# Attention and a quantised feed-forward layer on one core: the feed-forward work dealt between the attention steps of the next two batches

## The reference

```python
Q, K, V = (proj(Wq), proj(Wk), proj(Wv))              # einsum('oc,bct->bto'), split into heads
att = jnp.einsum('bhqd,bhkd->bhqk', Q, K) * (1.0 / math.sqrt(Dh)) + b[0]
att = att * m + (1.0 - m) * NEG_INF
att = jax.nn.softmax(att, axis=-1)
y = jnp.einsum('bhqk,bhkd->bhqd', att, V)             # transposed back to (B, C, T)
...
vals = NVFP4_LUT[idx] * scales                        # gate, up: [4096, 512], down: [512, 4096]
gate = jnp.einsum('th,nh->tn', xt, Wg)
up = jnp.einsum('th,nh->tn', xt, Wu)
gelu = jnp.tanh(0.7978845608028654 * (gate + 0.044715 * gate ** 3)) * gate * 0.5 + gate * 0.5
out = jnp.einsum('tn,hn->th', gelu * up, Wd)
return x + out.reshape(B, S, H)
```

## Time and profile before

| | us |
|---|---|
| median of three runs | 1612.29 |
| profiled execution, its own time | 1610.11 |
| span of its trace | 1608.3 |
| TensorE busy / VectorE / ScalarE / GpSimd | 1510.4 / 695.6 / 534.6 / 270.4 |
| mean granted TensorE clock | 0.937 |
| ScalarE table loads | 2, of 1283 ns |

### The profile page before, as it was taken

The page is one execution under the profiler, slowest core; times in us unless marked ns, Lnnn a source line. Parts: engine busy times, 40 slices in busy tenths (PEclk is TensorE's granted clock), DMA queues, the critical chain, the costliest instruction groups (busy, mean ns, idle before and its releaser), DMA issues.

```text
span 1608.3 us, 19482 instructions
## 1 busy us (share of the span) xinstructions
PE 1510.4 (94%) x7376; PEld 597.7 (37%) x7376; DVE 695.6 (43%) x1113; ACT 534.6 (33%) x701; POOL 270.4 (17%) x146
## 2 busy tenths in 40 slices
PE   3989889898989889999999999999999999999999
PEld 1222222222322224444444444444444444444444
DVE  5858676776777562323323233323233232122122
ACT  1447464564656463222222222222222222111111
POOL 2012112121211212122112212211221221000000
PEclk7779896897898899999999999999999999999999
DMA  5112221212221103001001000100100010000000
GB/s 165 44 51 59 65 63 43 61 44 57 67 69 42 51 21 124 20 20 40 20 20 33 26 20 20 39 20 20 36 23 20 20 39 1 0 26 26 0 26 26
DMA packets 32662, 63.04 MB, mean 39 GB/s; under 512 B 5584, under 2 KB 14928, under 8 KB 32480
## 3 DMA queue, kind: packets, MB, share of 16 engines
q1 hardware_dynamic: 29760, 59.42, 12.5%
q10 hardware_dynamic: 2848, 2.90, 0.5%
HBM read 49.43 MB, written 12.61 MB: 39 GB/s over the span
## 4 chain that ended last, share of the span: by engine, by line
PE 82%; DMA 6%; DVE 5%; SPq 3%; ACT 2%; issue 1%; ACTq 1%; POOL 1%; POOLq 0%; DVEq 0%
PE psum L828 14%; PE psum L830 14%; PE psum L829 14%; PE psum L769 7%; PE psum L899 7%; PE psum L901 7%; PE psum L900 7%; PE psum L798 6%; DMA wide<-seed_rows 4%; DVE maxima L638 3%; PE psum L784 3%; PE psum L756 2%; PE psum L805 1%; PE psum L746 1%; DMA wide<-max_lo 1%
## 5 line engine op out<-in xcount | busy, mean ns | idle before, releaser
L638 DVE TENSOR_REDUCE maxima<-psum 128x1 f32<-128x512 f32 x512 | 332.3, 685 | 161.9 <-PE psum L769 158.3
L703 DVE SCALAR_TENSOR_TENSOR small<-psum,small 128x512 f32<-128x512 f32 x128 | 88.5, 691 | 592.6 <-issue 306.6
L544 ACT ACTIVATE big<-psum 128x1024 f32<-128x1024 f32 x256 | 253.4, 1024 | 214.8 <-PE psum L784 198.2
L769 PE MATMUL psum<-wide 51*128 51x512 f16 x512 | 211.3, 447 | 68.3 <-DMA wide<-seed_rows 51.1
L580 ACT ACTIVATE small<-psum 128x512 f32<-128x512 f32 x128 | 76.4, 597 | 421.1 <-PE psum L830 421.1
L334 POOL TENSOR_TENSOR dq_w<-dq_code,dq_scales 128x1536 f32<-128x1536 f16 x32 | 109.8, 3433 | 541.8 <-DVE dq_code L371 541.8
L590 ACT CAST in_hi<-small 128x512 f16<-128x512 f32 x128 | 79.1, 618 | 361.8 <-DVE small L703 361.8
L828 PE MATMUL psum<-y_hi,wide 128*128 x512 | 194.1, 379 | 2.6 <-POOL wide L346 2.6
L828 PE MATMUL psum<-y_hi,w_even_hi 128*128 (+1 forms) x512 | 194.2, 379 | 1.2 <-POOL w_even_lo L346 1.2
L829 PE MATMUL psum<-y_lo,w_even_hi 128*128 (+1 forms) x512 | 194.0, 379 | 0.0
L830 PE MATMUL psum<-y_hi,w_even_lo 128*128 (+1 forms) x512 | 194.0, 379 | 0.0
(11 more groups left out here) (83 smaller groups left out, 1366.2 us busy)
## 6 DMA issues: line engine op xcount, KB each, us to landing
dq_packed<-packed SPq DMA_DIRECT2D x32, 384.0 KB
dq_scales<-scales SPq DMA_DIRECT2D x32, 384.0 KB
wide<-qk_parts SPq DMA_DIRECT2D x64, 128.0 KB
qk_parts<-wide SPq DMA_DIRECT2D x60, 128.0 KB
small<-x SPq DMA_DIRECT2D x8, 512.0 KB, 4.1
wide<-qk_parts SPq DMA_DIRECT2D x64, 64.0 KB
big<-x SPq DMA_DIRECT2D x4, 1024.0 KB, 9.5
out<-big SPq DMA_DIRECT2D x16, 256.0 KB, 2.1
```

The source lines that it names most:

```text
L544: nc.scalar.activation(p_exp[:, k, :, i], p_score[:, 2 * i:2 * i + 2, :], ACT.Exp, scale=SCORE_SCALE).then_inc(exp_done, 1)
L638: nc.vector.reduce_max(maxima[:, g % 2, n:n + 1], p_max[:, n % 2, :], AX.X).then_inc(max_red, 1)
L769: nc.tensor.matmul(p_max[:, n % 2, :], q_stack[rows, side, s, t * P:(t + 1) * P], k_stack[rows, side, s, :], start=True, stop=True).then_i ...
```

## The change

The FFN is no longer a stage of its own. It runs chunk by chunk (two batches), all 32 units for each chunk, and the FFN of chunk 0 lies among the attention steps of batches 2 and 3, chunk 1 among those of 4 and 5, chunk 2 among those of 6 and 7; chunk 3 comes after. `schedule()` deals the pieces: after each attention step of TensorE come as many FFN pieces (`G0`..`G3` gate, `U0`..`U3` up, `D` down, three matmuls each) as make the rest even. The first two spans hold 264 such steps each, and a chunk 368 to 400 pieces; a unit is 8 pieces, and every fourth unit carries 16 `D` pieces of down for the last four units. Batches 0 and 1 (`SOLO`) are as before.

With it: decoded weights are written to DRAM (`spill_unit`) during chunk 0, 30 units of which are decoded within that span, and read back for chunks 1 to 3 through a ring of eight units (`reload_unit`, 768 KB each); from batch 2 on the scores have one pair of banks in place of two, and gate and up one bank each; two `m` tiles, one in each half of the array, go together and are reduced in one instruction (`reduce_pair`); the low half of the product moves from VectorE to GpSimd (`inter_low`); SyncE loads two units at the start, and the first 1 MB of x rows for the sum after the first maxima.

```diff
-GROUPS = 4
-UNITS = F // P // GROUPS
+UNITS = F // P
+GROUP = 4
 CHUNKS = B * C // 512
+STEPS = CHUNKS * UNITS
+RING = 2 * GROUP
+IN_RING = GROUP + 1
+AHEAD_UNITS = 2
+LAST_CHUNK = (CHUNKS - 1) * UNITS
+LAST_SHARED = LAST_CHUNK // GROUP - 1
+SOLO = 2
...
-        y_hi = sb("y_hi", [P, TT, B * C], f16)
-        y_lo = sb("y_lo", [P, TT, B * C], f16)
-        w_even = [sb("w_even_hi", [P, UNITS, 2, WORDS], f16), sb("w_even_lo", [P, UNITS, 2, WORDS], f16)]
-        dq_packed = sb("dq_packed", [P, WORDS], u32)
-        dq_scales = sb("dq_scales", [P, WORDS], f32)
+        y_hi = sb("y_hi", [P, TT, 4 * C], f16)
+        y_lo = sb("y_lo", [P, TT, 4 * C], f16)
+        w_ring = sb("w_ring", [P, RING, 2, 2, WORDS], f16)
+        dq_packed = sb("dq_packed", [P, 2, WORDS], u32)
+        dq_scales = sb("dq_scales", [P, 2, WORDS], f32)
         dq_code = sb("dq_code", [P, WORDS], u32)
-        dq_sign = sb("dq_sign", [P, WORDS], u32)
-        dq_mag = sb("dq_mag", [P, WORDS], u32)
         dq_w = sb("dq_w", [P, 2, WORDS], f32)
+        w_dram = nc.dram_tensor("w_parts", [UNITS, P, 2, 2, WORDS], f16, kind="Internal").ap()
...
-        p_gate, p_up = [psum[:, 4, :], psum[:, 0, :]], [psum[:, 5, :], psum[:, 1, :]]
-        p_out = [psum[:, n, :] for n in (2, 3, 6, 7)]
+        def gate_bank(u):
+
+            return psum[:, 0 if u > LAST_CHUNK and u % 2 else 2, :]
+
+        def up_bank(u):
+
+            return psum[:, 1 if u > LAST_CHUNK and u % 2 else 3, :]
+
+        def out_bank(j, r):
+
+            return psum[:, 2 + r % 2 if j < LAST_SHARED else 4 + r, :]
...
+        def attention():
 
...
+        def ffn(c):
+
+            for u in range(UNITS * c, UNITS * (c + 1)):
+                for step in ("G0", "G1", "G2", "G3", "U0", "U1", "U2", "U3"):
+                    yield u, step, None
+                if u >= GROUP and u % GROUP == 0:
+                    for r in range(4):
+                        for i in range(GROUP):
+                            yield u, "D", (u // GROUP - 1, r, i)
+            if c == CHUNKS - 1:
+                for step in ("G0", "G1"):
+                    yield STEPS, step, None
+                for r in range(4):
+                    for i in range(GROUP):
+                        yield STEPS, "D", (STEPS // GROUP - 1, r, i)
+
+        def on_pe(step):
+
+            return step[0] in "SmAY" and step not in ("AO", "YN") or step == "MT" or step[0:2] in WORK and step[2] in "ab"
+
+        def schedule():
+
+
+            steps = list(attention())
+            ready = [n + 1 for n, (b, g, step, _) in enumerate(steps) if step == "YN" and g == 0 and b >= 2 and b % 2 == 0]
+            for b, g, step, arg in steps[:ready[0]]:
+                yield "attention", b, g, step, arg
+            for c in range(CHUNKS):
+                rest = list(ffn(c))
+                span = steps[ready[c]:ready[c + 1]] if c < CHUNKS - 1 else []
+                left = sum(on_pe(step) for _, _, step, _ in span)
+                for b, g, step, arg in span:
+                    yield "attention", b, g, step, arg
+                    if on_pe(step):
+                        count = len(rest) // left
+                        left -= 1
+                        for u, name, part in rest[:count]:
+                            yield "ffn", u, None, name, part
+                        rest = rest[count:]
+                for u, name, part in rest:
+                    yield "ffn", u, None, name, part
...
-        def weight_lo(pool, n, w, u):
+        def weight_hi(act, n):
+            if n >= RING:
+                group_free(act, n)
+                act.wait_ge(w_out[n % RING], 16 * (n // RING))
+            wait_apart(act, act_spare, w_f_s, n + 1)
+            nc.scalar.copy(w_ring[:, n % RING, 0], dq_w[:, :, :]).then_inc(w_hi_s, 1)
+
+        def weight_lo(pool, n):
             wait_apart(pool, pool_spare, w_hi_s, n + 1)
-            nc.gpsimd.tensor_tensor(unit_of(w[1], u), dq_w[:, :, :], unit_of(w[0], u),
+            nc.gpsimd.tensor_tensor(w_ring[:, n % RING, 1], dq_w[:, :, :], w_ring[:, n % RING, 0],
                                     ALU.subtract).then_inc(w_lo_s, 1)
 
-        def weight_hi(act, n, w, u):
-            wait_apart(act, act_spare, w_f_s, n + 1)
-            nc.scalar.copy(unit_of(w[0], u), dq_w[:, :, :]).then_inc(w_hi_s, 1)
...
+            def gelu_part(u):
+                act.wait_ge(gate_mm, u + 1)
+                wait_from(act, inter_s, u - 1)
+                nc.scalar.activation(gelu[:, u % 2, :], gate_bank(u), ACT.Gelu_apprx_tanh,
+                                     scale=1.0 / (Y_SCALE * W_SCALE)).then_inc(gelu_s, 1)
+
+            def inter_high(u):
+                act.wait_ge(inter_s, u + 1)
+                if u >= IN_RING:
+                    act.wait_ge(sum_mm, 4 * ((u - IN_RING) // GROUP + 1))
+                nc.scalar.copy(in_hi[:, u % IN_RING, :], inter[:, :]).then_inc(in_hi_s, 1)
+
+            for kind, b, g, step, arg in schedule():
+                if kind == "ffn":
+                    u = b
+                    if step == "G0" and u:
+                        inter_high(u - 1)
+                    elif step == "G1" and u + AHEAD_UNITS < UNITS:
+                        weight_scale(act, u + AHEAD_UNITS)
+                    elif step == "G2" and SOLO <= u + AHEAD_UNITS - 1 < UNITS:
+                        weight_hi(act, u + AHEAD_UNITS - 1)
+                    elif step == "G3":
+                        gelu_part(u)
+                    continue
+                q, first = 4 * b + g, b == 0
+                if step[0] == "S":
+                    k, i = int(step[1]), int(step[2])
+                    bank = 2 * i if b < SOLO else 0
+                    act.wait_ge(score_mm, 8 * q + 2 * k + i + 1)
+                    wait_from(act, av_done, 4 * q - 3 + k)
+                    nc.scalar.activation(p_exp[:, k, :, i], p_score[:, bank:bank + 2, :], ACT.Exp,
+                                         scale=SCORE_SCALE).then_inc(exp_done, 1)
...
+                column = 8 * (n % 2) + n // 2
+                nc.vector.reduce_max(maxima[:, g % 2, column:column + 1], p_max[:, n % 2, :], AX.X).then_inc(max_red, 1)
+
+            def reduce_pair(b, g, n):
+                q = 4 * b + g
+                if n == 0:
+                    wait_from(dve, max_t, q - 1)
+                dve.wait_ge(max_mm, 16 * q + n + 2)
+                nc.vector.reduce_max(maxima[:, g % 2, n // 2:n // 2 + 9:8], p_max, AX.X).then_inc(max_red, 2)
...
+            def inter_part(u):
+                dve.wait_ge(gelu_s, u + 1)
+                dve.wait_ge(up_mm, u + 1)
+                wait_from(dve, in_lo_s, u)
+                nc.vector.scalar_tensor_tensor(out=inter[:, :], in0=up_bank(u),
+                                               scalar=I_SCALE / (Y_SCALE * W_SCALE),
+                                               in1=gelu[:, u % 2, :], op0=ALU.mult, op1=ALU.mult).then_inc(inter_s, 1)
...
+                if b_now < SOLO or n % 2 == 0:
+                    wait_from(pe, max_red, 16 * (4 * b + g) + n - (1 if b_now < SOLO else 0))
+                e, i, t = n % 2, n // 8, n // 2 % 4
...
-                wait_from(pe, exp_done, n - 1)
+                wait_from(pe, exp_done, n - 1 if b < SOLO else n)
+                bank = 2 * i if b < SOLO else 0
                 for e in range(2):
                     rows, s = slice(HALF * e, HALF * e + STACK_ROWS), 2 * g + i
-                    last = nc.tensor.matmul(p_score[:, 2 * i + e, :], k_stack[rows, side, s, k * P:(k + 1) * P],
+                    last = nc.tensor.matmul(p_score[:, bank + e, :], k_stack[rows, side, s, k * P:(k + 1) * P],
...
+            def wait_bank(u, used, freed):
+
+                if u > LAST_CHUNK:
+                    wait_from(pe, freed, u - 1)
+                elif u > GROUP and u % GROUP == 1:
+                    pe.wait_ge(acc_add, 4 * (u // GROUP - 1) + used + 3)
+                    wait_from(pe, freed, u)
+
+            def gate(u, k):
+                if k == 0:
+                    if u % UNITS == 0:
+                        pe.wait_ge(y_lo_s, 8 * (u // UNITS) + 8)
+                    if u < UNITS:
+                        pe.wait_ge(w_lo_s, u + 1)
+                    else:
+                        pe.wait_ge(w_in[u % RING], 16 * (u // RING - UNITS // RING) + 16)
+                    wait_bank(u, 0, gelu_s)
+                last = three_products(gate_bank(u), u, 0, k)
+                if k == TT - 1:
+                    last.then_inc(gate_mm, 1)
+
+            def up(u, k):
+                if k == 0:
+                    wait_bank(u, 1, inter_s)
+                last = three_products(up_bank(u), u, 2 * P, k)
+                if k == TT - 1:
+                    last.then_inc(up_mm, 1)
+
+            def down(j, r, i):
+                u = GROUP * j + i
+                if i == 0:
+                    if r == 0:
+                        pe.wait_ge(in_lo_s, GROUP * j + GROUP)
+                    if j > LAST_SHARED:
```

(17 more changed lines are left out.)

503 lines of the change are left out of this document (217 added, 286 removed).

## The result

The changed kernel took **1632.98 us**, the median of four runs (1631.91 to 1634.31), beside 1614.82 for the kernel before, also a median of four; the ratio is 1.0122, 95% interval 1.0072 to 1.0171. It is slower by 1.2%, where 1594 was forecast. The profiled execution took 1631.91, its span is 1630.0, so the sum of 1592 missed by 38 us of span. The time lies inside the stated range of 1545 to 1645, but on the slower side, which had a chance of 0.22.

A forecast was written before the change was run, and what follows sets the result against it. The prediction took TensorE to bound the FFN, and TensorE and VectorE in turns attention; 1547 us without stalls plus 45 of stall gave 1592 of span, with 1.8 around it 1594 us, range 1545 to 1645.

The forecast's parts named there:

- the sum of 1592: Whole span: 1547 us without stalls plus 45 us of stall; with 1.8 us around it, 1594.
- TensorE's terms: TensorE's work over the whole kernel: FFN matmuls 993 us, attention steps after the shared part begins 323 us.
- The shared part: Attention and FFN dealt together: begins at 214 us, when the halves of y of batch 1 are there.
- The sum without stalls: Whole span with no stall at all: 1547 us, 61 us less than before.
- the 246 that the prediction named as a limit: Last chunk: taking more than its 246 us would show the prediction wrong.
- Spills, reloads, fills and `inter_low`: Weights' DMA traffic, stack fills and the product's low half on GpSimd: taken as covered, costed at nothing.
- the paragraph on GpSimd in chunk 0: Short units in chunk 0: weights' chain of 8.0 us against TensorE's 7.7 slips tenths, recovers in the fourth unit.
- The rival that named this place: Weights' chain paces chunk 0's short units: 14 us more than the forecast, 1608, no change; chance 0.10.
- The 45 us of stall: Shared chunks: TensorE waiting on ScalarE's ordered list, table loads and gate's banks, taken as 45 us; bounds nothing to 224.
- The exposed loads: Shared units: ScalarE's order shows one table load in each of 96, 123 us more, 1672, slower; chance 0.17.
- The doubled switch: ScalarE in the shared chunks: a table switch costs as much again as its load, 1796 or 1672; chance 0.05.
- theory V: From after the traces: in chunk 0 VectorE's decode and GpSimd's weights, looped and lengthening each other, cannot deliver each 7.7 us.

The follow-up runs named there:

- the kernel that has none of the disputed work: The changed kernel with VectorE's decode (from unit 2) and GpSimd's weights (from unit 8) on 64 of 768 words, tanh for gelu: 1551.72 us.
- the even deal with four early units: The changed kernel with weights' steps dealt separately, one unit per 12 FFN pieces, four units decoded in batches 0 and 1 instead of two: 1610.02 us.
- small decode: The changed kernel with VectorE's four decode operations on 64 of 768 words from unit 2 on: 1586.21 us; without table loads besides: 1569.18 us.
- the even one: The changed kernel with weights' steps dealt separately, one unit per 11 FFN pieces, two units decoded in batches 0 and 1: 1609.25 us; with tanh for gelu 1593.11.
- the two halves: The changed kernel with only VectorE's decode, or only GpSimd's two weights instructions, cut to 64 of 768 words: 1586.21 and 1582.42 us.
- Opening the loop alone: The changed kernel with the last decode step writing into the two-buffer `dq_packed`, so a decode does not wait for the weights before: 1624.17 us.

## Why the prediction was wrong

**TensorE's terms were right.** The shared part begins at 211.7 (214 forecast, and 4 more for DMAs at the start, of which the first `m` tile shows 0.5: 38.01 against 37.50). The sum without stalls, 1547, is 1551.6 in the kernel that has none of the disputed work, and with everything in place the last three chunks take 985 for 977. The trace after also has the prices themselves. From an `m` pair to the next piece it is 0.32 us, from the last matmul of a piece to an attention step 0.31, the pace of 0.2155 and 0.10 for the switch, and an `A` step takes 1.00:

```profile
522.41 0.38 PE L906 MATMUL psum<-y_hi,w_ring 128*128 128x512 f16 x1
522.73 0.39 PE L844 MATMUL psum<-wide 51*128 51x512 f16 x2
523.05 0.39 PE L904 MATMUL psum<-y_hi,w_ring 128*128 128x512 f16 x1
```

The last chunk takes 266.8 us, more than the 246 that the prediction named as a limit. That limit was wrong and not the sum: chunk 3 has 400 pieces, 259 us at 0.6465, with the end and the wait for y besides.

Spills, reloads, fills and `inter_low` were costed at nothing: in chunks 1 and 2 that stands, since no wait for them is listed. In chunk 0 it does not stand for `inter_low`, which is one of the operations beside which the decode stretches, though moving it away gave only 0.5 us in the even deal with four early units, where TensorE no longer waited for weights.

**The step that failed is the paragraph on GpSimd in chunk 0.** It took the weights of a unit as a chain of 8.0 us through one buffer, against 7.7 of TensorE, and said that it "recovers in the fourth"; "I count that within the 45". The chain is not the bound. It had left out VectorE's decode, as the whole prediction has no sum of VectorE's work in chunk 0 (0.95 + 0.55 + 0.55 + 0.95 = 3.0 us undisturbed), which is in a loop with `weight_f` through `dq_code`: L395 3.43 plus 3.0, if nothing intervenes, is only 6.4; but VectorE's steps hardly move while GpSimd runs L414 or L531. The exclusive time of the two is 3.43 + 3.10 + 1.16 + 3.0 = 10.7 us a unit, and the trace shows 10.4 to 13.4, 11.3 in the mean of the 22 turns of short units. They lose 22 x (11.3 - 7.7) = 79 us; chunk 0 was 81 too long. The rival that named this place had the price of 8.3, +14 us, and a chance of 0.10: right place, a sixth of the size. Its 14 us is close to what GpSimd's chain costs when the decode is small, 14.6; the rest comes from the pair.

**The 45 us of stall** had the wrong cause. It was put on ScalarE, its table loads above all; 1.2 us of chunk 0 hang on them, and all that TensorE waits for ScalarE is 18.0 us in chunk 0 (14.9 and 3.1) and 5.5 in the next two. That the measured time still lies in the range is luck: its upper part was meant for exposed loads. The 81 us taken apart, one step after the other, each from one profiled execution:

| step | chunk 0, us | difference |
|---|---|---|
| the sum without stalls | 352 | |
| small decode, small GpSimd weights, no loads | 364.2 | 12.2, with TensorE idle for 10.8 |
| GpSimd's weights back | 378.8 | 14.6 |
| the table loads back | 389.4 | 10.6 |
| VectorE's decode back | 433.2 | 43.8 |

The order matters: taken out first, the loads are worth 1.2, and with the decode out of the way 10.6. A wait behind the bound costs nothing until the bound is moved. By the way in which it comes about, against the kernel with none of it, 49 us are TensorE idle (59.4 against 10.8) and 20 are TensorE at a lower granted clock (373.8 us busy against 353.4, clock 0.94 against 0.99). So in this chunk the stall cost 1.4 times its idle time.

**The exposed loads,** the rival that gave 1672, was right in sign alone. The doubled switch fell: the load stands at 1.28 with nothing beside it. The page "ScalarE: Activation LUTs" of the Trainium skill, What ACT_TABLE_LOAD costs, has 2.66 us for a switch; no row of the two traces shows its drain, and with 175 loads taken away the whole gained 8.6 us in the changed kernel (7 by the ratios) and 16 in the even one, 0.04 to 0.09 us a load.

**What stays open.** The even kernel's chunk 0 is 57 us above 352: 9 go with the loads, some 11 are two waits for the stacks' DMAs, which were not tried apart, and the rest is spread over gelu, exponentials, weights and a clock of 0.96. That the two engines exclude each other is shown by durations and by the two halves; the exclusion itself could not be switched off. That moving whole operations between them changed nothing (396.0 for 393.7) is explained only by the waits, in which weights no longer stand; why theory V's 360 to 390 was missed, and what ScalarE's order costs there, has no experiment of its own with four early units.

## What to carry to other kernels

When work moves into a shorter stretch, add up for each unit not only what each engine does but what pairs of engines cannot do at once, and follow every buffer back to its next writer: nobody waited for the decode before, and it was part of the bound after. Opening the loop alone gave 8 of 81 us, since the two engines' times still added up. Compare the demand in its bursts, not in the mean: 433 us for 30 units is 14 us each, and the short units wanted one each 7.7. An extra cost on an engine that isn't the bound (80 us of table loads) can be nearly free, until the bound is removed.
